# A two-layer transformer kernel on one core: the first MLP strips of block 0 in two halves of 256 tokens

## The reference

```
h = ada_rms(x, cond, ln1_w, ln1_tw)           # x * rsqrt(mean(x^2) + eps) * w * (1 + cond @ tw.T), gain per sequence
q, k, v = h @ Wq.T, h @ Wk.T, h @ Wv.T        # 8 query heads, 1 key/value head, head size 64, rotary positions
x = x + softmax(q k / 8) v @ Wo.T             # attention inside each sequence of 64 tokens
h = ada_rms(x, cond, ln2_w, ln2_tw)
x = x + (silu(h @ Wg.T) * (h @ Wu.T)) @ Wd.T  # inner width 2048
```

## Time and profile before

| | |
|---|---|
| median of 3 runs | 2566.2 us (2564.31 to 2566.88) |
| the profiled execution's own time | 2565.41 us |
| its span | 2563.5 us |
| TensorE busy | 2502.4 us, 98% of the span |
| VectorE, ACT, GpSimd busy | 1392.8, 960.8, 1065.0 us |
| chain that ended last | TensorE 85%, VectorE 4%, GpSimd 4% |

### The profile page before, as it was taken

How to read it: one execution, slowest core, us unless ns; L and a number is a source line. 1 busy time by engine, 2 the same in 40 slices (tenths; PEclk the granted TensorE clock), 3 DMA queues, 4 the chain that set the end, 5 groups by cost and what they waited for, 6 DMA issues and landing times.

```text
span 2563.5 us, 47440 instructions
## 1 busy us (share of the span) xinstructions
PE 2502.4 (98%) x18502; PEld 1261.3 (49%) x18502; DVE 1392.8 (54%) x2150; ACT 960.8 (37%) x1560; POOL 1065.0 (42%) x1007
## 2 busy tenths in 40 slices
PE   7799999999999999999999999999999999999999
PEld 5445444454444544445454445554545455454544
DVE  7574343443434434344486575766757576775752
ACT  4352232322323223232343452635445262634542
POOL 3342222322223222232354455655556465654632
PEclk8999999999999999999999999999999999999999
DMA  6420101001010010100322412121121212111110
GB/s 220 170 73 18 39 3 49 8 17 40 3 50 7 17 39 3 50 7 15 120 83 82 129 31 77 28 60 43 52 67 30 80 26 72 43 51 55 30 63 29
DMA packets 113115, 133.30 MB, mean 52 GB/s; under 512 B 44686, under 2 KB 56078, under 8 KB 112916
## 3 DMA queue, kind: packets, MB, share of 16 engines
q1 hardware_dynamic: 112916, 130.26, 16.7%
HBM read 75.83 MB, written 18.74 MB: 37 GB/s over the span
## 4 chain that ended last, share of the span: by engine, by line
PE 85%; DVE 4%; POOL 4%; issue 3%; ACT 2%; DMA 1%; SPq 0%; POOLq 0%; DVEq 0%; ACTq 0%
PE ps_m L1588 47%; PE ps_abef L1588 19%; PE ps_d L1588 2%; PE ps_c L1588 2%; PE ps_abef L1797 2%; PE ps_abef L1790 2%; PE ps_abef L1792 2%; PE ps_abef L1826 1%; PE ps_d L1776 1%; PE ps_c L1642 1%; PE ps_abef L1834 1%; POOL inner L932 1%; PE ps_abef L1815 1%; POOL scratch L960 1%; PE ps_d L1689 1%
## 5 line engine op out<-in xcount | busy, mean ns | idle before, releaser
L1588 PE MATMUL ps_m<-h_mlp,weights 128*128 128x512 f16 x3168 | 726.8, 381 | 11.5 <-issue 5.0
L1588 PE MATMUL ps_m<-weights,inner 128*128 128x512 f16 x3072 | 693.8, 379 | 2.1 <-DVE scratch L1421 2.1
L1588 PEld LDWEIGHTS ps_m<-h_mlp,weights 128*128 128x128 f16 x3168 | 305.0, 98 | 360.3 <-issue 14.6
L932 POOL TENSOR_TENSOR inner<-scratch,inner 128x512 f16<-128x512 f32 x256 | 314.0, 1227 | 393.0 <-ACT inner L1117 392.8
L1588 PEld LDWEIGHTS ps_m<-weights,inner 128*128 128x128 f16 x3072 | 296.0, 98 | 336.1 <-issue 4.0
L1588 PE MATMUL ps_abef<-h_mlp,weights 128*128 128x512 f16 x1440 | 332.2, 379 | 0.0
L1117 ACT CAST inner<-scratch 128x512 f16<-128x512 f32 x256 | 157.0, 613 | 154.3 <-DVE scratch L1421 84.7
L1588 PEld LDWEIGHTS ps_abef<-h_mlp,weights 128*128 128x128 f16 x1440 | 136.5, 98 | 156.1 <-issue 4.2
L910 POOL TENSOR_TENSOR h_mlp<-scratch,h_mlp 128x512 f16<-128x512 f32 x64 | 74.0, 1156 | 191.4 <-ACT h_mlp L1072 191.4
L972 POOL TENSOR_TENSOR scratch<-scratch 128x512 f32<-128x512 f32 x64 | 72.6, 1134 | 163.3 <-DVE scratch L1475 163.3
L1072 ACT CAST h_mlp<-scratch 128x512 f16<-128x512 f32 x64 | 39.5, 618 | 262.3 <-POOL scratch L972 141.8
(11 more groups left out here) (173 smaller groups left out, 3673.2 us busy)
## 6 DMA issues: line engine op xcount, KB each, us to landing
x_mlp<-x_attn SPq DMA_DIRECT2D x64, 256.0 KB, 2.3
scratch<-scratch SPq DMA_DIRECT2D x128, 128.0 KB, 2.7
weights<-gamma SPq DMA_DIRECT2D x128, 128.0 KB, 2.9
x_attn<-x SPq DMA_DIRECT2D x32, 256.0 KB, 2.7
x_mid<-x_mlp SPq DMA_DIRECT2D x32, 256.0 KB, 2.3
x_attn<-x_mid SPq DMA_DIRECT2D x32, 256.0 KB, 2.7
out<-x_mlp SPq DMA_DIRECT2D x32, 256.0 KB, 2.2
inner<-wada_t SPq DMA_DIRECT2D x4, 1024.0 KB, 8.5
```

The lines of the kernel that those rows point to most:

```text
L932: nc.gpsimd.tensor_tensor(inner[:, 1, j, :], src, inner[:, 0, j, :], ALU.subtract).then_inc(L.m_lo, 1)
L1588: ins = nc.tensor.matmul(o, left(a, k), right(b, k), start=(first and n == 0), stop=(last and n == len(order) - 1), skip_group_check=True)
```

## The change

`HALVES` is 8. The first eight strips of block 0 are computed in two halves of 256 tokens. The first halves (tokens 0 to 255, `early`) get six stages of their own, `gate_h, up_h, tanh_h, gated_h, m_hi_h, m_lo_h`, put into `FIRST0` at the planned times `HALF0_AT`. The second halves stay in `START0`, on the other 256 columns (`columns`). `with_mlp` counts half a pass for these strips. `START0` gets lags of its own (`LAGS0S`) and is now walked by TensorE and GpSimd too. The semaphores `up`, `act`, `gated`, `m32`, `m_hi` and `m_lo` of layer 0 count 8 more from there on. TensorE waits for `m32` to reach 8 ahead of `block0`. The two stores of the gains of layer 0 count on `s_gain_st`, for which `tanh_h` 0 waits; the wait ahead of tanh 0 for all stores goes. The high part of a norm of block 0 no longer waits for `up`. `NORM0F`, `CHAIN0F`, `FIRST0_STARTS`, `FIRST0_SECOND`, `SETUP0` and `SETUP_START0` have new planned times, and with them another order in both lists.

```diff
-FIRST0_STARTS, FIRST0_SECOND = [10.3, 25.0, 39.8, 54.6], [46.3, 61.2, 76.7, 184.5]
+FIRST0_STARTS, FIRST0_SECOND = [9.9, 24.7, 39.5, 57.1], [47.1, 65.6, 83.2, 162.2]
 SETUP_START0 = [
-    (0.2, "cut", "gate2"), (3.6, "load", "down1"), (6.8, "cut", "up2"), (12.6, "cut", "gate3"), (21.2, "cut", "up3"),
-    (24.2, "load", "down0"), (26.7, "cut", "down0"), (28.8, "load", "down2"), (45.5, "cut", "down1"),
-    (45.5, "cut", "down2"), (56.3, "cut", "down3"), (65.3, "load", "down3")]
+    (0.1, "cut", "gate2"), (2.1, "cut", "up2"), (2.5, "cut", "gate3"), (3.6, "load", "down1"), (8.3, "cut", "up3"),
+    (9.9, "load", "down0"), (12.4, "cut", "down0"), (15.3, "cut", "down1"), (25.2, "cut", "down2"),
+    (28.3, "cut", "down3"), (35.7, "load", "down2"), (37.2, "load", "down3")]
+HALVES, HALF0_AT = 8, [80.2, 86.4, 134.7, 150.1, 158.0, 160.2, 161.7, 301.2]
+HALF0 = [("gate_h", 0.0), ("up_h", 1.4), ("tanh_h", 2.9), ("gated_h", 3.4), ("m_hi_h", 4.5), ("m_lo_h", 5.0)]
+LAGS0S = {"up": [("tanh", -0.2), ("gated", 0.8), ("m_hi", 3.0), ("m_lo", 6.1)], "down": LAGS0["down"]}
...
+        def columns(it, j):
+
+            return slice(BLOCK // 2 if first_block(it) and j < HALVES else 0, BLOCK)
+
+        early = slice(0, BLOCK // 2)
...
+            def half_mlp(stage, j):          # VectorE
+                if stage == "gated_h":
+                    g = act0[:, j % 2, early]
+                    dve.wait_ge(L0.act, j + 1)
+                    nc.vector.scalar_tensor_tensor(g, g, 1.0, ps_m[2 * (j % 2)][:, early], ALU.add, ALU.mult).then_inc(L0.gated, 1)
+                    dve.wait_ge(L0.gated, j + 1)
+                    dve.wait_ge(L0.up, j + 1)
+                    nc.vector.scalar_tensor_tensor(g, g, 0.5 * INV * INV, ps_m[2 * (j % 2) + 1][:, early], ALU.mult,
+                                                   ALU.mult).then_inc(L0.m32, 1)
...
+            def half_mlp(stage, j):          # TensorE
+                if stage == "gate_h":
+                    if j == 0:
+                        pe.wait_ge(s_ada_out, len(ADAS))
+                        pe.wait_ge(L0.h_lo, max(norm_no(NORMS0F, 0, "norm2", t) for t in range(TILES // 2)) + 1)
+                    if j >= 2:
+                        pe.wait_ge(L0.m32, j - 1)
+                    if j % 4 == 0:
+                        pe.wait_ge(s_wlo, cut_no(no_of(f"up{j // 4}")))
+                    products([(ps_m[2 * (j % 2)][:, early], lambda b, k: h_mlp[:, b, k, early])],
+                             lambda a, k: gate_w[:, a, k, P * j:P * (j + 1)], range(KC))
+                if stage == "up_h":
+                    products([(ps_m[2 * (j % 2) + 1][:, early], lambda b, k: h_mlp[:, b, k, early])],
+                             lambda a, k: up_w[:, a, k, P * j:P * (j + 1)], range(KC)).then_inc(L0.up, 1)
...
-            pe.wait_ge(s_ada_out, len(ADAS))
+            pe.wait_ge(L0.m32, HALVES)
...
-            block0(0, True)
+            block0(0, START0, True)
```

More of the change, by code:

```diff
@@ L79, in emit @@
             merged.append((now, "gamma_m", j))
-        now += PASS3
+        now += PASS3 * (0.5 if kind in ("gate", "up") and j < halves else 1.0)
         if k == (IC if kind == "down" else KC) - 1:
@@ L141 @@
     ("turn_p", 29.9), ("c_lo", 29.9), ("key_major", 30.3), ("c_hi", 30.9), ("mix", 32.5), ("out", 35.3), ("add", 37.9)]
-NORM0F = list(zip([s for s, _ in NORM0], [0.0, 0.2, -1.3, 3.9, 2.9, 4.7, 5.1]))
+NORM0F = list(zip([s for s, _ in NORM0], [0.0, 1.9, 2.1, 6.2, 3.4, 6.6, 4.7]))
 CHAIN0F = [(s + "1", at) for s, at in NORM0F] + [
-    ("rot", 6.0), ("proj", 8.4), ("qk_lo", 8.6), ("qk_hi", 10.0), ("spread", 11.9), ("feature_major", 17.1),
-    ("turn", 17.3), ("p_lo", 17.3), ("scores", 17.4), ("shift", 17.4), ("soft", 17.8), ("exp", 19.3), ("p_hi", 19.9),
-    ("key_major", 23.8), ("c_hi", 23.9), ("turn_p", 24.1), ("c_lo", 24.4), ("mix", 24.8), ("add", 26.6), ("out", 29.1)]
+    ("rot", 10.2), ("proj", 11.9), ("qk_lo", 11.9), ("qk_hi", 13.0), ("feature_major", 16.5), ("turn", 18.1),
+    ("spread", 18.3), ("shift", 20.1), ("scores", 20.7), ("soft", 21.0), ("exp", 21.7), ("p_hi", 26.0), ("p_lo", 26.4),
+    ("key_major", 27.0), ("c_lo", 29.6), ("turn_p", 29.7), ("c_hi", 30.3), ("mix", 32.2), ("add", 32.8), ("out", 33.9)]
 PE_COST0 = {"turn_x1": 0.45, "turn_x2": 0.45, "proj": 3.3, "turn": 0.6, "scores": 0.5, "turn_p": 0.5, "mix": 0.9, "out": 2.6}
@@ L165 @@
-SETUP_START0 = [
[3 rows of a table removed]
+    (1.5, "load", "up0"), (2.2, "sin", 0), (4.7, "ang", 0), (5.5, "load", "ada4"), (7.5, "ang", 1), (8.4, "rope", 0),
+    (9.0, "load", "ada5"), (10.1, "load", "gate0"), (12.4, "cut", "qkv"), (12.7, "ada", 0), (13.8, "sin", 1),
+    (14.0, "cut", "qkv_v"), (16.1, "load", "ada2"), (17.1, "ang", 2), (20.8, "cut", "wo"), (22.4, "sin", 2),
+    (24.6, "ada", 1), (26.5, "consts", 0), (27.1, "rope", 1), (27.9, "load", "ada6"), (28.5, "rows", 0),
+    (30.2, "rope", 2), (31.4, "ada_out", 1), (33.0, "cut", "gate0"), (35.7, "ada", 4), (36.3, "load", "ada7"),
@@ new lines @@
+    (36.9, "ang", 3), (42.0, "ada", 5), (44.3, "sin", 3), (44.6, "rope_out", 0), (47.0, "ada", 6), (49.3, "rope", 3),
+    (50.4, "load", "ada3"), (50.5, "load", "gate2"), (56.0, "ada", 7), (60.6, "cut", "up0"), (62.7, "ada_out", 0),
+    (62.9, "load", "up2"), (63.0, "ada", 2), (63.8, "load", "gate1"), (64.1, "ada_out", 5), (66.3, "bias", 0),
+    (68.9, "ada", 3), (70.4, "bias", 1), (72.1, "bias", 2), (80.3, "cut", "gate1"), (80.4, "ada_out", 2),
+    (82.4, "ada_out", 4), (87.6, "load", "up1"), (88.0, "ada_out", 6), (104.5, "ada_out", 7), (123.2, "cut", "up1"),
@@ L1064, in norm_hi @@
                 else:
-                    act.wait_ge(L.up, it * IC)
+                    if not first_block(it):
+                        act.wait_ge(L.up, strips_before(L) + it * IC)
                     if first_block(it):
@@ L1874, in _ @@
                         else:
[L1875 removed]
+                            pe.wait_ge(L0.gated, HALVES + it * IC + j)
                     ins = products([(ps_m[0][:], lambda b, k: h_mlp[:, b, k, :])],
```

134 lines of the change are left out of this document (74 added, 60 removed).

## The result

| | before | after |
|---|---|---|
| median (lowest to highest) of 20 runs each | 2565.44 us (2562.83 to 2569.07) | 2571.94 us (2566.95 to 2573.39) |
| the profiled execution's own time, its span | 2565.41, 2563.5 us | 2572.25, 2570.4 us |
| TensorE busy | 2502.4 us | 2506.4 us |

The ratio is 1.0023, 95% interval 1.0016 to 1.0030: the changed kernel is 6.5 us slower. The forecast was 2568 us and no change. The time lies inside the range, but it is the time of rival L, late attention (2572.2), and the cause is partly the one it names.

What follows compares the result with a forecast made beforehand. TensorE, fully busy in layer 0's repeated part, left only its loss ahead of block 1 to win: start at 121.6 plus a 161.3 us pass, then 2.1 slow start, gave +2.0 us; forecast 2568 us, range 2557 to 2577.

Steps and rivals of the forecast that it cites:

- rival L: Block 0's attention does not come forward, held by its tile chains; scores of tile 3 still at 95, 2572.2 us; chance 0.20.
- S: Start of START0's first full-list gate product, 120.02 before; forecast 121.6, bounds 118 to 126.
- N: Start of block 1's first gate product, 283.07 before; forecast 282.9, sign 281 to 287.
- A: Block 0's attention up to scores of tile 3: they end at 91 instead of 95, with 3 to 5 us of waits left.
- B: Scores to end of tile 3's projection: 7.2 us to the turned probabilities, then 5.4; ends at 104, 8.5 us earlier.
- D: The START0 pass: 139.1 us of TensorE work plus stalls, 161.3 in sum against 163.05 before.
- C: Strips 2 to 7 after tile 3's projection, a turn, and a new 1.45 us wait for the last strip's multiplying-out.
- D1: Before gate 2 in the START0 pass: TensorE waits 5.0 us behind three VectorE cuts; bounds 3.5 to 7.
- D2: Behind the wait before gate 2: TensorE restarts at half speed, costing 2.0 us.
- D6: End of the START0 pass: second norms of tiles 2 and 3 leave TensorE idle 9.75 us; bounds 8 to 12.
- D3: Before gates 4, 5 and 8: cuts up3, down0 and down1 in VectorE's way, 2.1 us; bounds 0 to 5.
- rival P: VectorE and GpSimd share a port: three START0 cuts wait for subtractions, +3.5 us, 2571.7; chance 0.10.

Runs made afterwards that it cites:

- The last experiment: Two-strip kernel with six start-up products, with modulation products 2 and 3 moved behind tile 3's scores and the early strips behind its output product: 2560.18 us, ratio 0.9984.
- cuts apart: Changed kernel with the planned times of five weight cuts in block 0's pass moved so that each stands between two strips' products: 2577.23 us, ratio 1.0043.
- 118 start-up products: Changed kernel with 118 instead of 54 start-up products of the identity on TensorE: 2571.61 us, ratio 1.0023.
- one-pass kernel: Changed kernel with the earlier START0 list and one of three passes of every gate, up and down product in that list: 2541.70 us, ratio 0.9907.
- old order: Changed kernel with eight early strips kept, but block 0's pass walking the START0 list of before: 2565.27 us, ratio 1.0002.
- list alone: Changed kernel with the new FIRST0 but no early strips, and START0 as before: 2561.92 us, ratio 0.9988.
- mended: Load of up0, angles and rotation of the last table part moved in the first list: changed kernel 2572.15 us; kernel with the new first list only 2563.54 us.
- two strips with six: Kernel with two early strips and START0 as before, with 6 instead of 54 start-up products: 2558.74 us, ratio 0.9975.
- four strips: Changed kernel with four early strips instead of eight, START0 as before and 86 start-up products: 2564.02 us, ratio 0.9991.
- two strips: Changed kernel with two early strips instead of eight and START0 as before, 54 start-up products: 2584.20 us, ratio 1.0078.
- before with 102: Kernel before the change with 102 instead of 54 start-up products, nothing else: 2589.50 us, ratio 1.0089.

## Why the prediction was partly right

**By its own signs the prediction failed up to S and held behind it.** It called itself wrong if S lay outside 118 to 126, and S is 128.64. Scores of tile 3 were to end before 93 (95.3), the projection before 106 (110.93), and N to lie at 281 to 287 (289.95). The signs inside the pass held: 4.53 us before gate 2, 2.22 before down 0, 9.3 before block 1. That the time came out near is in part luck: N moved by 6.9 us, and by the prediction's rule (N's move, and 2.1 for the slow start) the time should have grown by 9.0, to 2574.4. It grew by 6.5, since stretches behind N gave some of it back.

**A failed, 4.3 us.** Scores of tile 3 end at 95.3, not at 91. I had seen 14.2 us of idle time for 7.1 us of products and took the rest for slack that the attention could move into. The idle time did take the products, to the microsecond (busy 40.82 to 48.58), and the scores stayed where they were. The step that failed is the walk through the new order: it left 3 to 5 us of waits between 40 and 95, and 6.4 are left there (55.00 less 48.58). The last experiment shows that two things hold the scores: the two modulation products cost them 2.8 us of their 7.3, and for the rest the tile chains over ACT, VectorE and GpSimd hold them. Moving the three entries that showed waits only moved the waits. This is rival L by its point of decision, 94.1, and in part by its mechanism, since TensorE's own products hold the scores too.

**B was half right.** The wait is 7.5 us (7.2 foreseen), and this is the whole gain of the new list. But the strips under it leave 3.38 us open, and behind them turn, half strip, mix and turn run at half speed or near it: to the projection's end 8.15 us instead of 5.4. The prediction charged a slow start behind the two longest idle times in D and forgot this one: 2.75 us. It isn't there in every profile: with the cuts apart and with 118 start-up products, the same instructions behind the same wait of 3.38 ran at full speed (granted 1.00, 5.8 us to the projection's end). What decides it is open, and it accounts for most of the 3.3 and 2.6 us by which S came earlier in these two profiles.

**C held.** 110.93 to 128.64 is 17.7 us against 17.6, with the new wait at 1.39 (1.45). S is 7 us later than forecast through A and B alone.

**D held in its sum, 161.31 against 161.3, and in its large terms**: D1 4.53 (5.0), D2 with the 18 products behind it 3.64 instead of 1.97, so 1.7 (2.0), D4 2.22 (2.2), D5 0.48 (1.2), D6 1.77 + 4.83 + 2.74 = 9.3 (9.75). D3 did not come as forecast: of its 2.1 us of waits for cuts 0.19 came, and the other wait there, 1.18 at 155.09, is a turn that waits for GpSimd's low part, as one did for 1.11 in the pass before. All these waits make 19.6 us where 22.2 were forecast. TensorE's own time makes up for it, 143.2 busy where 139.1 and D2's 1.7 were forecast, so the exact sum is luck. Block 1's first turn then takes 161.87, 2.1 over the 159.76 of before, as the forecast's 2.1, but for two reasons: 1.4 of it is the slow start and 0.56 the idle time at the turn, which nobody forecast. What I concluded from D1 afterwards, to spread the cuts, was wrong: of the two orders tried, in a row is the cheaper one.

**What bounds the pass.** The forecast found the stalls but not their reason. Taking 20.7 us of products out of a pass in which attention had been hidden behind them uncovers the attention, and the cuts of weights that stand in and beside its chain: the one-pass kernel's pass is 26 us shorter for 69 us less work, the old order's 5.2 for 20.7, the new order's 1.7. That the attention alone would hold the pass is shown only for the one-pass kernel, behind its last cut. The order can choose where the gap shows, in the middle or at the end, and the end is 3.4 us dearer in the pass and 1.5 more in block 1's slow start. By the ratios, each good to some 2 us, the new START0 order costs 5.4 us, the early strips with the old order cost 3.6, and the new first list brings 3.1. These are steps from one kernel to the next, so they add up to the 5.9 us of the ratio by construction and are no test of it.

**Behind N.** The prediction said that nothing changes there. The difference grows from 6.9 us at N to 11.0 at the end of the layer-0 loop and is back at 7.0 at the last turn of layer 1's loop. Block 1 adds 2.1 us and the rest of layer 0's loop 2.0, with 2.1 us of idle time at its turns in all. Layer 1's loop gives back 3.2: four of its turns had 2.3 us of idle time without a releaser before and two have 0.4 now, and a wait of 0.94 for VectorE at another is gone. The remaining 0.8, between the two loops, I haven't explained: that stretch takes 345.8 to 349.5 us in the kernels measured here, which have the same code there. For the changed kernel the place cost nothing in the end; a shift of 48 products would have cost some 24.

## What to carry to other kernels

Before moving work into idle time, ask what the work was hiding where it stood: the gap that it leaves is filled only if the chain beside it has slack. Look also at what else, here the cuts of weights, stands in that chain's way on the other engines. Idle time inside a chain takes other work without making the chain faster; what a list can win there is read from the one wait that ends last, not from the sum of the idle time. And when a small edit ahead of a loop gives an answer that its own stretch can't explain, compare the turns of the loop, and vary the number of instructions ahead of it before judging the edit.

## What the runs showed of the hardware

A hardware loop on TensorE can have idle time at its turn that depends on how many products stand ahead of it in the program. Products ahead of the layer-0 loop, counted against the kernel before, idle time without a releaser at a turn of that loop, and a turn's length:

| products ahead | kernels | idle at a layer-0 turn | layer-0 turn | layer-1 turn |
|---|---|---|---|---|
| 0 | before; list alone, also mended; two strips with six, also with modulation behind | 0 (once 0.21) | 159.8 to 160.0 | 146.8 to 147.6 |
| +128, +256 | four strips; changed with 118 | 0 (once 0.16) | 159.8 to 160.1 | 146.7 to 147.3 |
| +192, -192 | changed, also old order, cuts apart, mended; one pass | 0.35 to 0.63 | 160.3 to 160.6 | 146.4 to 147.0 |
| +48 | two strips; before with 102 | 2.7 to 3.5, then half speed in 8 of 10 | 163.2 to 166.2 | 146.4 to 146.8 |

(Without block 1 itself and the last turn of either loop, which end on other things.) The places 0, +128 and +256 behave alike, and so do +192 and -192: these six places fit a cost that repeats after 128 products. Other instructions ahead of the loop, such as waits on semaphores, aren't counted, and some of these kernels differ in them. The Trainium skill, page "Runtime: NRT & Kernel Launch", section "Instruction fetch mechanics", states that an engine's instructions are fetched in blocks of 256 and that a taken branch whose target isn't in the current window of two such blocks must wait for a transfer. A product is a weight load and a multiplication (the kernel before has 18502 of each), so 128 products are 256 instructions, and the runs agree with the page's block; that the wait is such a transfer no run here shows directly. Layer 1's loop behaves the other way round at these places: its turns are shortest at +48, +192 and -192. Why +48 costs several times as much as +192 stays open; other distances weren't tried.

Two steps meet at the fourth cut of START0: VectorE's takes 2.29 us, as the one at 131.48 with no step of GpSimd beside it, and GpSimd's subtraction of 128x256 beside it 2.48, where the one ahead of it took 0.67.

```profile
142.63 2.29 DVE L1300 SCALAR_TENSOR_TENSOR weights<-weights 128x2048 f16<-128x2048 f32 x1 [1.23 <-ACT weights L1049]
```

```profile
141.40 0.67 POOL L947 TENSOR_TENSOR inner<-scratch,inner 128x256 f16<-128x256 f32 x1
142.97 2.48 POOL L947 TENSOR_TENSOR inner<-scratch,inner 128x256 f16<-128x256 f32 x1 [0.89 <-ACT inner L1153]
```

It is GpSimd that waits, and the cut isn't longer: the 3.5 us of rival P, in which cuts wait for subtractions, did not come in the changed kernel, whose longest cut took 2.46. A cut can be the longer one: with the old START0 order one of 3.24 was seen (the second of the pair at 172.27). In the kernel before, the changed one and the one with the old order it is mostly GpSimd's low parts that grow beside cuts, and where TensorE waits for them, as at 178.06 with the old order, that is part of the price.
